# The state-space phase of a decoder kernel: products on GpSimd by time, factors and sums by TensorE's transpose mode, scans in pieces

## The reference, cut to what matters

```python
def _selective_scan(u, A_log, D, x_proj_w, dt_proj_w, dt_proj_b):
    A = -jnp.exp(A_log)
    x_dbl = u @ x_proj_w.T
    dt, Bm, Cm = jnp.split(x_dbl, [DT_RANK, DT_RANK + D_STATE], axis=-1)
    delta = jax.nn.softplus(dt @ dt_proj_w.T + dt_proj_b)
    dA = jnp.exp(delta[..., None] * A)
    dBu = delta[..., None] * Bm[:, :, None, :] * u[..., None]
    def step(h, inp):
        dA_t, dBu_t, C_t = inp
        h = dA_t * h + dBu_t
        y = jnp.einsum('bdn,bn->bd', h, C_t)
        return (h, y)
    ...
    return y + u * D
```

## Time and profile before

| | us |
|---|---|
| median of 3 runs | 2929.82 (2928.88 to 2934.28) |
| profiled execution, its time | 2930.72 |
| profiled execution, its span | 2929.0 |
| VectorE busy, share of the span | 1966.5, 67% |
| TensorE busy | 2444.2, 83% |
| ScalarE busy | 1627.9, 56% |
| GpSimd busy | 1088.4, 37% |

### The profile page before, as it was taken

The page is one execution under the profiler, slowest core; times in us unless marked ns, Lnnn a source line. Parts: engine busy times, 40 slices in busy tenths (PEclk is TensorE's granted clock), DMA queues, the critical chain, the costliest instruction groups (busy, mean ns, idle before and its releaser), DMA issues. The chain is left out here.

```text
span 2929.0 us, 48455 instructions
## 1 busy us (share of the span) xinstructions
PE 2444.2 (83%) x16333; PEld 1819.3 (62%) x16335; DVE 1966.5 (67%) x3626; ACT 1627.9 (56%) x4541; POOL 1088.4 (37%) x1547
## 2 busy tenths in 40 slices
PE   4888989884996999989964996999997769989396
PEld 3666767663984666656632774666665547756385
DVE  5999999992324666656789363777776347767355
ACT  6776767751224777765554334778775346645011
POOL 3454876843551111102221312222220055523654
PEclk8999898986997999999985997999998979999598
DMA  8400000002752000000004000000000000000276
GB/s 343 195 1 1 8 8 6 10 5 97 213 148 68 2 2 1 2 8 1 1 9 62 10 1 18 2 1 1 1 1 9 17 1 1 1 9 15 89 205 199
DMA packets 73974, 129.77 MB, mean 44 GB/s; under 512 B 29113, under 2 KB 47361, under 8 KB 69634
## 3 DMA queue, kind: packets, MB, share of 16 engines
q1 hardware_dynamic: 62210, 103.46, 11.6%
q0 software_dynamic: 9216, 19.02, 1.8%
q10 hardware_dynamic: 2304, 4.20, 0.4%
HBM read 69.23 MB, written 57.41 MB: 43 GB/s over the span
## 5 line engine op out<-in xcount | busy, mean ns | idle before, releaser
L871 DVE TENSOR_TENSOR_SCAN s_state<-s_decay,s_state 128x4096 f32<-128x4096 f32 x32 | 278.0, 8687 | 1.7
L760 PE MATMUL s_ysumP<-s_state,ident 128*128 128x256 f32 x1024 | 258.2, 401 | 0.0
L1790 ACT ACTIVATE s5a_prob<-s5a_scoreP,s5a_nmax 128x256 f32<-128x256 f32 x512 | 235.5, 481 | 22.7 <-DVE s5a_nmax L1970 21.0
L608 ACT ACTIVATE s_decay<-s_delta,s_aneg 128x255 f32<-128x255 f32 x512 | 211.8, 494 | 51.9 <-POOL s_delta L438 51.5
L1790 ACT ACTIVATE s2s_prob<-s2s_scoreP,s2s_nmax 128x128 f32<-128x128 f32 (+1 forms) x512 | 208.2, 425 | 42.2 <-DVE s2s_nmax L1968 38.1
L760 PEld LDWEIGHTS s_ysumP<-s_state,ident 128*128 128x128 f32 x1024 | 203.1, 205 | 29.5
L3551 POOL DMA_INDIRECT parts<-m_y,m_to x160 | 153.1, 957 | 134.7 <-DVE m_y L3642 109.7
L1970 DVE TENSOR_REDUCE s5a_nmax<-s5a_scoreP 128x4 f32<-128x1024 f32 x128 | 156.1, 1220 | 67.0 <-PE s5a_scoreP L1891 64.7
L668 PE MATMUL s_bcP<-s_bc,s_sel 96*128 96x256 bf16 x768 | 133.5, 313 | 65.0 <-DVE s_state L881 45.5
L1968 DVE TENSOR_REDUCE s2s_nmax<-s2s_scoreP 128x2 f32<-128x256 f32 (+1 forms) x256 | 130.0, 549 | 75.9 <-PE s2s_scoreP L1886 73.7
L1981 DVE TENSOR_TENSOR s5a_probT<-s5a_probP,s5a_mask 128x768 f32<-128x768 f32 x128 | 122.5, 957 | 62.8 <-PE s5a_probP L1901 61.7
(11 more groups left out here) (645 smaller groups left out, 6137.1 us busy)
## 6 DMA issues: line engine op xcount, KB each, us to landing
sorted<-blank SPq DMA_DIRECT2D x32, 1105.0 KB, 27.9
m_w<-in_m_w SPq DMA_DIRECT2D x40, 512.0 KB, 4.2
m_w<-in_m_w SPq DMA_DIRECT2D x40, 384.0 KB, 3.9
m_xin<-sorted SPq DMA_DIRECT2D x80, 130.0 KB, 2.7
m_back<-parts SPq DMA_DIRECT2D x16, 256.0 KB, 6.6
m_back<-parts ACTq DMA_DIRECT2D x16, 256.0 KB, 7.2
s4w_mats<-s_scratch SPq DMA_DIRECT2D x4, 1024.0 KB, 12.7
parts<-m_y,m_to POOLq DMA_INDIRECT x160, 3.4
```

The costliest lines, as they stand in the source:

```text
L608: ins = nc.scalar.activation(decay[c][:, n, 1:], delta[:, c, 1:], ACT.Exp, scale=aneg[:, c, n:n + 1])
L760: ins = nc.tensor.matmul(ysumP[:, c, :], ident[:], state[s][:, c, n, :], start=False, stop=(n == NS - 1))
L871: nc.vector.tensor_tensor_scan(cells, flat(decay[c]), cells, 0.0, ALU.mult, ALU.add).then_inc(S["scanned"], 1)
L1790: ins = nc.scalar.activation(prob[i][:, h, a:b], scoreP[i][:, h, a:b], ACT.Exp, bias=nmax[:, p % 4, h, r:r + 1], accum_out=den[s][:, r, 2 ...
```

## The change

- **Input products** move from VectorE to GpSimd and are made with time on the partitions: `turn_du` transposes `du` on TensorE, `duT_in` copies it to SBUF, `weigh` multiplies it by the B column of a state, and `feed` transposes the product back into PSUM (`inP`), two states a call, where the scan reads it.
- **Scans** go in pieces of two states and one half, 16 of 128x512 a batch, through a ring of three state tiles.
- **The factors C** are spread by transposing a column that is broadcast over 128 columns (`spread`); the bf16 parts and `sel` go.
- **State sums** are made by transposes that add in PSUM (`sums`), so `ysumP` has time on the partitions; `gate` works there, and `turn_y` and `yT_in` turn the result back.
- `part` of softplus goes from two ScalarE instructions to one on GpSimd. The lists of all engines are written anew around the 8 pieces; `slots` goes to the start of the next batch, `choose` behind the first piece.

```diff
-    NS, GN = 16, 4
-    NG = NS // GN
+    NS, NP = 16, 8
+    CH = 2 * NP
+    RING = 3
...
-            def split(t, s):
...
+            def weigh(t, s, p):
+                if p == 0:
+                    pool.wait_ge(S["duT_ready"], t + 1)
+                    pool.wait_ge(S["bct_ready"], t + 1)
+                wait(pool, S["fed"], CH * (t - 1) + 2 * p + 2)
+                for n in (2 * p, 2 * p + 1):
+                    for g in range(TB):
+                        ins = nc.gpsimd.tensor_scalar(wb[:, n, g, :], duT[:, g, :], bct[s][:, g, n:n + 1], None, ALU.mult)
+                ins.then_inc(S["wb_ready"], 1)
             def lost_part(t):
-                pool.wait_ge(S["kept_part"], 2 * t + 2)
+                pool.wait_ge(S["em_ready"], t + 1)
+                st.do(nc.gpsimd.tensor_scalar(part[:], em[:], 1.0, -1.0, ALU.add, ALU.add))
                 st.do(nc.gpsimd.tensor_tensor(lost[:], em[:], part[:], ALU.subtract))
...
# GpSimd, batch t
+                for p in range(4):
+                    weigh(t, s, p)
                 if more:
-                    front(t + 1)
                     grow(t + 1)
+                for p in range(4, 6):
+                    weigh(t, s, p)
                 if lot is not None and k < 3:
                     sets(lot, 3 * k, 3 * k + 2)
+                for p in range(6, NP):
+                    weigh(t, s, p)
+                if t + 2 < NB:
+                    front(t + 2)
                 if more:
-                    split(t + 1, 1 - s)
                     lost_part(t + 1)
                     steps_in(t + 1, 1 - s)
...
# ScalarE, batch t
+                decays(t, 0)
+                duT_in(t)
...
+                decays(t, 5)
+                if more:
+                    front(t + 1, 1 - s)
+                    steps_out(t + 1, 1 - s)
+                decays(t, 6)
+                if t >= 1:
+                    size_out(t - 1)
+                decays(t, 7)
+                if more:
+                    soft(t + 1)
+                if t >= 2:
+                    rows_in(t - 2)
+                if more:
+                    logarithm(t + 1)
...
# TensorE
+            def feed(t, s, k):
+                i = CH * t + k
+                wait(pe, S["scanned"], i - 2)
+                pe.wait_ge(S["wb_ready"], NP * t + k // 2 + 1)
+                c = k % 2
+                for a in range(2):
+                    for g in range(TB):
+                        ins = nc.tensor.transpose(inP[i % 3][:, a, g * P:(g + 1) * P],
+                                                  wb[:, k // 2 * 2 + a, g, c * P:(c + 1) * P], ident[:])
+                ins.then_inc(S["fed"], 1)
+            def spread(t, s, p):
+                wait(pe, S["prodded"], 2 * (NP * t + p))
...
+                        ins = nc.tensor.transpose(cP[:, a, g * P:(g + 1) * P],
+                                                  bct[s][:, g, n:n + 1].to_broadcast([P, P]), ident[:])
+            def sums(t, s, p, c):
+                pe.wait_ge(S["prodded"], 2 * (NP * t + p) + c + 1)
+                r = (NP * t + p) % RING
+                for a in range(2):
+                    for g in range(TB):
+                        ins = nc.tensor.matmul(ysumP[:, g, c * P:(c + 1) * P], state[r][:, c, a, g * P:(g + 1) * P], ident[:],
+                                               start=False, stop=(p == NP - 1 and a == 1), is_transpose=True, skip_group_check=True)
+            def turn_du(t):
+                pe.wait_ge(S["mag_ready"], 4 * t + 4)
+                pe.wait_ge(S["du_ready"], t + 1)
...
# TensorE, batch t: for p in range(NP)
+                    if p < NP - 1:
+                        feed(t, s, 2 * p + 2)
+                    ...
+                        sums(t, s, p - 1, 0)
+                    spread(t, s, p)
+                        sums(t, s, p - 1, 1)
+                        feed(t, s, 2 * p + 3)
+                    if p == 0:
+                        turn_in(t + 1, 1 - s)
+                        skip(t, s)
+                    elif p == 1:
+                        turn_y(t - 1, min(t + 1, NB - 1))
+                        conv_in(t + 1, 1 - s, 0)
+                    elif p == 2:
+                        carry(t - 1, 1 - s)
+                        conv_in(t + 1, 1 - s, 1)
+                    elif p == 3:
+                        res_in(t + 1, 1 - s)
+                        out(t - 1)
+                    elif p == 4:
+                        dbl_out(t + 1, 1 - s)
+                    elif p == 5:
+                        pre_out(t + 1, 1 - s)
+                        turn_rows(t - 2)
+                    elif p == 7:
+                        gates(t - 2)
+                        turn_du(t + 1)
+                        feed(t + 1, 1 - s, 0)
+                        feed(t + 1, 1 - s, 1)
+                        ranks(routed(t))
...
# VectorE
+            def scan(t, s, p, c):
+                i = NP * t + p
+                ve.wait_ge(S["decayed"], 2 * i + c + 1)
+                wait(ve, S["summed"], 2 * (i - RING) + c + 1)
+                ve.wait_ge(S["fed"], 2 * i + c + 1)
+                nc.vector.tensor_tensor_scan(flat(state[i % RING][:, c]), flat(decay[c][:, 2 * p:2 * p + 2, :]),
+                                             flat(inP[(2 * i + c) % 3][:]), 0.0, ALU.mult, ALU.add).then_inc(S["scanned"], 1)
+            def outputs(t, s, p, c):
+                ve.wait_ge(S["c_ready"], i + 1)
+                nc.vector.tensor_tensor(part, part, cP[:], ALU.mult).then_inc(S["prodded"], 1)
...
+                for p in range(NP):
+                    scan(t, s, p, 0)
+                    scan(t, s, p, 1)
+                    if p == 0 and t > 0:
+                        gate(t - 1, 1 - s)
+                    outputs(t, s, p, 0)
+                    outputs(t, s, p, 1)
+                    if p == 0 and routed(t) is not None:
+                        choose(routed(t))
```

More of the change, by code:

```diff
@@ L360, in row2 @@
             return buf[:, i, :] if isinstance(i, int) else buf[:, bass.ds(i, 1), :].rearrange("p a c -> p (a c)")
-        def batches(eng):
-            for j in turns(eng, NB // 2, last=7):
-                for s in range(2):
-                    yield 2 * j + s, s, not (isinstance(j, int) and j == NB // 2 - 1 and s == 1)
         def routed(t):
-            return (t - 6) // 4 if isinstance(t, int) and t in (6, 10, 14) else None
+            return (t - 6) // 4 if t in (6, 10, 14) else None
         LOADED = 16 * 14
@@ L451, in _ @@
             grow(0)
[L452 removed]
+            front(1)
             lost_part(0)
@@ L658, in _ @@
             pe.wait_ge(S["zeroed"], 3)
-            def spread(t, s, k):
-                r = t * SP + k
-                wait(pe, S["bc_used"], r - 1)
-                if k == 0:
-                    pe.wait_ge(S["bc3_ready"], t + 1)
-                line = GN * k if k < 2 * NG else GN * (k - NG)
-                for n in range(GN):
-                    ins = nc.tensor.matmul(bcP[k % 2][:, n, :], sel[:, line + n, :], bc3[s][:], start=True, stop=True)
-                ins.then_inc(S["bc_ready"], 1)
@@ L678, in front_in @@
-                if isinstance(t, int) and t == 0:
-                    pe.wait_ge(S["weights"], LOADED)
-                    pe.wait_ge(S["taps"], 1)
-                wait(pe, S["delta_ready"], t)
-                for c in range(2):
-                    for k in range(TAPS):
-                        ins = nc.tensor.matmul(xmP[:, c, :], wtap[:, k, c * P:(c + 1) * P], xnT[:, k:k + L],
-                                               start=(k == 0), stop=(k == TAPS - 1))
-                ins.then_inc(S["projected"], 1)
@@ L687, in front_in, with conv_in @@
-                wait(pe, S["sres_ready"], t)
-                for c in range(2):
-                    ins = nc.tensor.matmul(resP[:, c, :], win[:, 256 + c * P:256 + (c + 1) * P], xnT[:, TAPS - 1:],
+            def conv_in(t, s, c):
+                if c == 0:
+                    pe.wait_ge(S["xnT_ready"], t + 1)
+                    if t == 0:
+                        pe.wait_ge(S["weights"], LOADED)
+                        pe.wait_ge(S["taps"], 1)
+                    wait(pe, S["duT_ready"], t)
+                for k in range(TAPS):
+                    ins = nc.tensor.matmul(xmP[:, c, :], wtap[:, k, c * P:(c + 1) * P], xnT[:, k:k + L],
+                                           start=(k == 0), stop=(k == TAPS - 1))
+                if c == 1:
+                    ins.then_inc(S["projected"], 1)
@@ L812, in _ @@
+            for c in range(2):
+                sums(NB - 1, 1, NP - 1, c)
+            turn_y(NB - 1, NB - 1)
             turn_rows(NB - 2)
```

358 lines of the change are left out of this document (160 added, 198 removed).

## The result

The changed kernel takes 3071.68 us (median of four runs, 3067.58 to 3075.22) against 2932.02 (2928.88 to 2934.28) for the kernel before, run beside it: 1.0477 times as long, with a 95% interval of 1.0458 to 1.0495. The direction was forecast; the size was not: 2985 was said, with 3055 as the upper end. The profiled executions of `final_tt` and `lean_choose`, two kernels further down, took 46 and 41 us more than the median of their runs, but this does not lie in the phase read here: batches 1 to 5 have the same mean interval in `final_tt` as in `final_ts` (39.06), and the last batch of `lean_choose` starts 13.9 us before that of `lean`, where the medians are 12.3 apart.

A forecast was written before the change was run, and what follows sets the result against it. A loop on TensorE, ScalarE and GpSimd through the next batch's front and `du` sets the period: 45.0 + 15 x 41.0 + 36 + 36.1 = 732.1 against 676.6, +55.5, so 2985 us; own range 2955 to 3010, reaching 2905 to 3055.

The forecast's parts named there:

- The step that failed: GpSimd's tensor_scalar, priced without a row: 0.40 us for 128x256 (`weigh`), 0.6 for 128x512 (`part`), 1.27 at the other end.
- Last link: From the copy `duT_in` to the next first scan, through `weigh` 0 and `feed`: forecast 2.8 us.
- the first link: From a batch's first scan to the end of `dbl_out`, through TensorE's pieces 0 to 4: forecast 22.7 us.
- Rival (d): GpSimd's tensor_scalar costs what two inputs cost: +1.3 at `weigh` 0, +0.65 at `part`, 2.0 a batch, 3015 us; chance 0.14.
- GpSimd's sum: Per batch, 32 `weigh` at 0.40 are 12.8 us, the rest about 12; at 0.73 the sum is 35, no bound.
- The loop through the front: Next batch's front on TensorE, ScalarE, GpSimd, then `du`, `weigh`, `feed`: sets the period, 41.0 us with clock loss.
- The 5.5 for `ranks` and `slots`: In routed batches, 4.12 of waiting for ranks and 1.1 of slots are felt before the next scan: 5.5 us more.
- The lock: VectorE instructions with two SBUF inputs shut out GpSimd's; should be gone, `lost` at 1.3 us against 8.95.
- Rival (b): TensorE's transposes overlap better than 0.11, say half: period 36.3, 2909 us, or 2895 with no clock loss; chance 0.16.
- rival (a): TensorE loses no clock: period 38.4, +6, 2935 us; chance 0.12.
- Rival (c): TensorE's low clock stays through transposes: 3260 us throughout, 3030 if until the taps of piece 1 and 2; chance 0.14.
- The clock's term: TensorE's waits for `du` cost clock: +0.9 for turning and feeding, 1.7 behind the first scan, +2.6 us a batch.

The follow-up runs named there:

- final_tt: `both_warm` with VectorE making `part` before piece 6 instead of before piece 7; ratio 1.0094 to the kernel before.
- lean_choose: `lean` with `choose` behind the last output product of its batch, `ranks` behind the next feeds, `shares` in the next batch; ratio 0.9975.
- final_ts: `final_tt` with GpSimd's products of pieces 2 to 7 as tensor_scalar again; ratio 1.0061 to the kernel before.
- lean: `final_ts` without the 20 identity products ahead of `turn_du`, the 6 behind it kept; ratio 1.0033 to the kernel before.
- warm_tr: Changed kernel with `feed` 2 behind the sums in piece 0 and 44 and 34 identity transposes in TensorE's two waits; ratio 1.0348.
- both: Changed kernel with broadcast products, `weigh` 0 and 1 and `part` on VectorE, `dbl_out` early, `ranks` ahead of `turn_du`; 2971.65 us, ratio 1.0130.
- both_warm: `both` with 20 identity products ahead of `turn_du` and 6 ahead of the first feed; 2959.24 us, ratio 1.0087.
- the last kernel: `lean_choose` with ScalarE's copy of the logits moved behind `duT_in` of the next batch; ratio 0.9943 to the kernel before.
- run 512: Not a follow-up run: the words are part of "run 512 times", the count of `weigh` products on GpSimd in the changed kernel; no time of its own.

## Why the prediction was wrong in size

The forecast for the end of the phase was 732.1, measured 813.0: +80.9. By its own terms: first scan of batch 0 at 49.4 and not 45.0, +4.4; fifteen intervals 5.06 longer, +75.9; routing and DMAs 33.2 and not 36, -2.8; the end 39.5 and not 36.1, +3.4. The rest of the kernel and the two medians add about 6. Of the first term, 1.7 us go with the tensor_tensor form of `weigh` and 1.3 with `part` on VectorE, where the first scan came at 47.67 and 48.05. The +3.4 of the end was not taken apart; one visible piece is `out`, 1.92 us at a clock of 0.50, where 1.06 was counted.

**The step that failed** is a price: "With one input it is nearest to the copy". A tensor_scalar of 128x256 on GpSimd took 0.92, not 0.40, and not even between the ends that I had set, 0.40 and 0.73 of the earlier trace rows; `part` took 1.94 where 1.27 was the upper end. The two rows were operations of another kind, and a bound from them was none. It entered in three places, of which I had two. Last link: `weigh` 0, +2.3. `part`: +1.3. And the first link: my chain held `weigh` 0 only, but `feed` 2 stands first in TensorE's piece 0 and waits for `weigh` 1, with the gate's sums behind it; at 0.40 a product it would have been ready, at 0.92 it is not: +1.9, of which the run with `feed` 2 moved gives back 1.7. Rival (d) was the right mechanism, with 30 us for 81.

**GpSimd's sum** was worked out as 24.8 us, 35 at most, and called no bound. In the window of one batch it is 39.98 of 46.4, and in batches that send rows it delays the chain. The runs with a higher clock (0.4 a batch) and with `dbl_out` early (nothing in four batches) show it.

**What held.** The loop through the front, `du`, `weigh` and `feed` sets the interval: each link shortened alone moved it by about as much (`part`, the least exact, by 1.05 for 1.39). The 5.5 for `ranks` and `slots` (4.12 and 1.1 are 5.2, so the sum was slightly off) came out as 5.7, the last link of a routed batch being 10.83 against 5.10. VectorE ceased to be the bound and is idle 9.5 to 13 us ahead of each batch, but for those that `slots` opens. The lock is gone: `lost` takes 1271 ns on the mean, where the median was 8945; a scan with one input in PSUM leaves GpSimd free. The Trainium skill (SBUF — State Buffer, Who interferes with whom) says that a VectorE instruction with at most one SBUF input, outside the 2-port modes, does not contend with GpSimd; by these numbers the trace agrees. Rival (b) fell: four transposes start 0.44 before the next four (239.12, 239.56), 0.11 each. So did rival (a), since the clock is at 0.50 after both waits. Rival (c) fell too: the clock is low for the first 7 us of a batch, the upper bound that I had priced, and then transposes run at full clock. Transposes alone even brought it back: between its fall at 221.2 and its rise at 238.2 TensorE did nothing but transposes, 34 of them:

```profile
221.20:238.20 17.00, 7.72 (x34) 7.00 (x35) 3.33 (x4) 7.33 (x19) 15.93 (x20) 0.50 0.01 1
238.20:240.00 1.80, 1.80 (x19) 1.80 (x18) 1.80 (x3) 1.57 (x5) 1.80 (x3) 0.99 0.00 0
```

And in `warm_tr` nothing but transposes filled the stretch from 212 to 216, the clock there was 1.00, and `turn_du` and the feeds behind it ran at full clock. The Trainium skill (TensorE: Matmul & The Clock Gate, Part 4: PE-mode transpose) has the rule that the full clock does not engage for transposes; these traces do not bear it out. The clock's term was forecast as 2.6 a batch and measured as 1.9 (`both` against `both_warm`), where no other wait hid it.

**Where the expected gain is.** The change does free VectorE. Its gain appears once `weigh` 0 and 1, `part`, `dbl_out`, `choose` and the copy of the logits no longer stand in the chain: 35.6 us a batch without routing against 37.8, and 38.0 against 39.0 on the mean of all fifteen intervals. What stays open is the batches that send rows: whether cheaper products on GpSimd (the broadcast form of `weigh` on top of the last kernel) would shorten them was not tried.

## What to carry to other kernels

A price that no row shows is not bounded by rows of other operations on the same engine: where an instruction is to run 512 times, the range should hold double the nearest row (0.92 against 0.40 here), and the order of the work around it has to be checked at that price too (which list entry waits for the second piece, not only the first). When work moves to an idle engine, add up that engine's whole batch with its upper prices before calling it free. And a cover for a wait (identity products, a step moved for its due time) is cut for one timing of its neighbours: after each edit that shortens the chain, look again at what now stands ahead of it; the last 2 us here lay in a copy that had been harmless in its place until the chain was short.

## What the runs showed of the hardware

- GpSimd, float32: tensor_scalar with a factor for each partition, 128x256: 0.92 us; with two constants, 128x512: 1.94; tensor_tensor 128x512 with one operand broadcast: 1.04, against 1.27 with two full ones. The form with fewer inputs was the dearer. On VectorE `part` took 0.42, and products of 128x256 from PSUM followed each other by 0.40.
- GpSimd's issue of an indirect DMA of first rows and of second rows took 1.03 and 0.96 us on the mean of the phase in the changed kernel, 2.20 and 1.87 before. Before, seven of these issues took 8.35 to 8.87 us, and each of the seven overlapped one of the scans of 8.69.
- VectorE's small SBUF operations are stretched beside GpSimd's tensor_tensor: in `both`, `choose`:

```profile
293.66 0.97 DVE L991 SCALAR_TENSOR_TENSOR s_conv<-s_conv,s_col 128x64 f32<-128x64 f32 x1
...
297.17 0.22 DVE L991 SCALAR_TENSOR_TENSOR s_conv<-s_conv,s_col 128x64 f32<-128x64 f32 x1
```

The same line, with the same shape, took 0.97 while GpSimd made its 128x512 tensor_tensor products (they ended at 296.5) and 0.22 afterwards. Beside GpSimd's tensor_scalar it took 0.38 (`final_ts`).
